# A decoder layer on one core: the rotary halves of the token totals are mixed before the token sum, by GpSimd and VectorE, instead of after it, by TensorE

## The chip, the cores and the metric

The kernel runs on one core of one Trainium2 chip. The metric is device time in microseconds; the figure compared is a median of several runs. The core has a matrix engine (TensorE, PE in the profile, with its weight loads shown apart as PEld), VectorE (DVE), ScalarE (ACT), GpSimd (POOL) and SyncE (SP), which only issues transfers. The engines run their own instruction streams in order and meet at semaphores.

## The reference, cut to what matters

The program is one decoder layer over 4 batches of 512 tokens and 512 features: an attention-like block, a second product with a context, and a feed-forward block with experts. The part that the change touches is in the first block:

```
Xn = layernorm(X) * gamma + beta
Q, K, V = split(Xn @ W_in + b_in)                 # 512 features each
K, V = rotary(K), rotary(V)                       # on the first 256 features
A = sum over tokens of (K/|K|) * (V/|V|)          # one vector of 512 per batch
Y = (0.5 * A + 0.5) * Q                           # the same A for every token
out = Y @ W_out + b_out + X
```

The rotation turns neighbouring features (2m, 2m+1) into each other. The product of a rotated K and a rotated V, element by element, is for a pair: half the sum of the two plain products, plus or minus half of a term that contains the cosine and sine of twice the angle. So a plain product and a "rotated" term are summed over the tokens, and the pair is mixed once per batch instead of once per token.

## The kernel before, in words

The program has two stages. The first (up to about 211 us of the profile) makes K, V, Q, the vector A and the attention output of the four batches, then one maximum over everything; the second does the context product and the feed-forward part. The change is in the first stage.

Every large product in it is done as three products of split numbers (high times high, high times low, low times high), of 512 columns each. Per batch b of the first stage TensorE's order, written out by hand, is: K and V of the four token tiles 0 to 3 (`key_value`, lines 898 to 928; each of the four steps k of a tile is six products at lines 908 and 914), four query products c = 0 to 3 of 12 matmuls (`query`, lines 864 to 866) with transposes of the next batch between them, and the four attention output tiles of the batch before (`attention`). After batch 3 there are the attention tiles of batch 2, then query 0 to 3 of batch 3 (line 1065), and the attention tiles of batch 3. Queries 0 and 2 write the same PSUM bank, as do 1 and 3: query(b, c) for c of 2 or 3 waits until ScalarE has copied query(b, c - 2) out (line 954).

The token totals. For each token tile VectorE adds a bias to K and V (`add_kv_bias`, lines 640 and 641), ScalarE sums squares (line 418), GpSimd makes a weight from them (`weight`, lines 319 and 321), and VectorE forms five products (`products`, lines 657 to 665): 512 plain ones and 256 rotated ones. Tile 0 writes them into `total` (128 x 768), the others into `prod`, and GpSimd starts a transfer that adds `prod` to `total` (line 328). In the last batch VectorE does the last of these additions itself (`last_total`, line 671). Before products(b, 0) overwrites `total`, it waits until the token sum of batch b - 1 is done (line 654).

The token sum and the mixing. TensorE sums `total` over its 128 partitions with six small products against a column of ones (line 940), two or three at a time between the steps of other products: for batch 0 after the first and the second step of K/V tile 2 of batch 1 (line 1036), for batches 1 and 2 after the third and the fourth step of K/V tile 1 of the next batch (line 1029), for batch 3 within query 2 (line 965). ScalarE copies the six columns out (`copy_sums`, line 424), and three more small products against constant matrices mix the pairs (`mix_sums`, lines 948 to 950): ahead of K/V tile 3 of the next batch, in batch 3 inside query 3. VectorE makes the multiplier `amul` from that (line 675), ScalarE makes the high half of Y with it (`high_y`, line 441), VectorE the low half (`low_y`, line 681).

VectorE's order in batch b = 1 is: add_kv_bias(1, 0), next_stats(2), ctx_amax(1), add_kv_bias(1, 1), products(1, 0), normalise of batch 2, add_kv_bias(1, 2), products(1, 1), ctx_amax(2), multiplier(0), low_y(0, 0 to 3), add_kv_bias(1, 3), products(1, 2) and (1, 3). ScalarE's is: the squares of tiles 0 and 1, copy_sums(0), the squares of tile 2, high_y(0, 0 to 3), query(1, 0), query(1, 1), the squares of tile 3, query(1, 2).

Of the kernel before, what the change touches and what calls it, by code (L numbers as in the profile page):

```python
# [23 lines left out]
P = 128  # L24
B, S, D = 4, 512, 512
KC = D // P
CHUNKS = (D + D // 2) // P
# [23 lines left out]
C_ID, C_MIX, C_IOTA, C_TRIG = 0, P, 4 * P, 4 * P + TOPK  # L51
# [3 lines left out]
def shape_constants():  # L55

    c = np.zeros((P, C_ALL), np.float32)
    c[:, C_ID:C_ID + P] = np.eye(P)
    i = np.arange(P)
    pair = (i[:, None] // 2 == i[None, :] // 2).astype(np.float64)  # L60
    even = (i % 2 == 0)
    c[:, C_MIX:C_MIX + P] = 0.5 * pair
    c[:, C_MIX + P:C_MIX + 2 * P] = np.where(np.eye(P) > 0, 0.5, -0.5 * pair)
# [27 lines left out]
def decoder_layer(nc, x, ctx, mask, w_in, b_in, w_out, b_out, gamma, beta, w_q, keys, down_embed, up_embed,  # L91
# [14 lines left out]
    with ExitStack() as whole:  # L106
# [57 lines left out]
        with ExitStack() as first:  # L164
# [18 lines left out]
            mix = sb("mix", [P, 2, P], F32)  # L183
# [8 lines left out]
            ones_col = sb("ones_col", [P, 1], F32)  # L192
            rsum = sb("rsum", [P, 8], F32)
# [18 lines left out]
            total_all, total_in, rsum_done, mix_mm, amul_done = sem("total_all"), sem("total_in"), sem("rsum_done"), sem("mix_mm"), sem("amul_done")  # L212
# [39 lines left out]
            def _(sp):  # L252
# [17 lines left out]
                sp.dma_start(mix[:].rearrange("p a b -> p (a b)"), consts[:, C_MIX:C_MIX + 2 * P]).then_inc(s_const, 16)  # L270
# [21 lines left out]
            def _(pool):  # L292
# [3 lines left out]
                nc.gpsimd.memset(ones_col[:], 1.0).then_inc(s_pool_const, 1)  # L296
                nc.gpsimd.memset(ones_sq[:], 1.0).then_inc(s_pool_const, 1)
                pool.wait_ge(s_pool_const, 4)
# [75 lines left out]
            def _(act):  # L374
# [45 lines left out]
                def copy_sums(b):  # L420
                    act.wait_ge(asum_mm, b + 1)
                    if b:
                        act.wait_ge(mix_mm, b)
                    nc.scalar.activation(rsum[:, 0:6], ob[0][:, 0:6], ACT.Copy).then_inc(rsum_done, 1)

# [39 lines left out]
                for b in range(B):  # L465
# [59 lines left out]
                copy_sums(LAST)  # L525
# [16 lines left out]
            def _(dve):  # L542
# [319 lines left out]
            def _(pe):  # L862
# [67 lines left out]
                def token_sums(b, chunks):  # L930

                    if b == LAST:
                        pe.wait_ge(z_done, TB * (b - 1) + 3)
                    if b == LAST:
                        pe.wait_ge(total_all, 1)
                    else:
                        pe.wait_ge(total_in, 16 * 3 * (b + 1))
                        pe.wait_ge(prod_done, TB * b + 1)
                    for c in chunks:
                        last = nc.tensor.matmul(ob[0][:, c:c + 1], total[:, c * P:(c + 1) * P], ones_col[:], start=(c == 0), stop=(c == CHUNKS - 1), skip_group_check=True)  # L940
                    if c == CHUNKS - 1:
                        last.then_inc(asum_mm, 1)

                def mix_sums(b):
                    if b == LAST:
                        pe.wait_ge(z_done, TB * (b - 1) + 4)
                    pe.wait_ge(rsum_done, b + 1)
                    nc.tensor.matmul(ob[1][:, 0:2], mix[:, 0], rsum[:, 0:2], start=True, stop=False, skip_group_check=True)
                    nc.tensor.matmul(ob[1][:, 0:2], mix[:, 1], rsum[:, 4:6], start=False, stop=False, skip_group_check=True)
                    nc.tensor.matmul(ob[1][:, 2:4], ident[:], rsum[:, 2:4], start=False, stop=True, skip_group_check=True).then_inc(mix_mm, 1)  # L950

                def query(b, c, sums=None, mix_of=None):
# [10 lines left out]
                    for k in range(KC):  # L963
                        if sums is not None and k:
                            token_sums(sums, range(2 * k - 2, 2 * k))
                        if mix_of is not None and k == 1:
                            mix_sums(mix_of)
# [3 lines left out]
                def attention(b, i):  # L971
# [5 lines left out]
                    elif i >= 2:  # L977
                        pe.wait_ge(*((rsum_done, b + 1), (amul_done, b + 1))[i - 2])
# [41 lines left out]
                pe.wait_ge(s_const, 32)  # L1020
                pe.wait_ge(s_pool_const, 4)
                for b in range(B):
                    if b:
                        first_key_value(b)
                        for i in range(1, 2):
                            for k in range(KC):
                                key_value(b, i, k)
                                if b > 1 and k >= 2:
                                    token_sums(b - 1, range(3 * (k - 2), 3 * (k - 1)))
# [9 lines left out]
                    if b:  # L1039
# [28 lines left out]
                query(LAST, 3, mix_of=LAST)  # L1068
# [25 lines left out]
        with ExitStack() as second:  # L1094
# [199 lines left out]
            def _(pool):  # L1294
                own = Steps(pool, s_psteps)
                own.base, own.n = 0, TB * B
# [783 lines left out]
```

## Time and profile before

| what | value |
|---|---|
| time, median of 3 runs | 791.81 us (791.77 to 791.91) |
| span of the profiled execution, first to last instruction | 789.7 us |
| TensorE busy | 774.6 us, 98% of the span |
| VectorE busy | 663.4 us, 84% |
| ScalarE busy | 322.7 us, 41% |
| GpSimd busy | 357.4 us, 45% |
| mean granted TensorE clock | 0.997 |

The profile shows one execution. Of that execution its span is given, and no time of its own beside it; the span lies 2.1 us under the median of the runs. Rows of a timeline give start in us, duration in us, engine, line, operation, output and inputs with shapes, a count of merged instructions, and in brackets how long the engine had been idle before and what released it. A float32 product that is not in the split form counts as two matmuls (the six small products of a token sum show as x12).

### The profile page before, as it was taken

The numbers are of one execution on the slowest core, as the hardware profiler recorded it, in microseconds if no ns is written. First come the engines' busy times: TensorE is split into PE (matmuls) and PEld (weight loads), VectorE is DVE, ScalarE is ACT, GpSimd is POOL, SyncE is SP. The second block draws the span as 40 slices with busy tenths as digits, with TensorE's granted clock in tenths as the row PEclk, the third lists the DMA queues.
The fourth block names the chain that finished last, engine by engine and source line by source line (L and its number), as shares of the span: only waits on it lengthen the run. The fifth ranks groups of instructions, "written<-read, shape, count | busy, mean of one in ns | idle before, by whom it ended". The sixth has DMA issues, their size and how long they took to land.

```text
span 789.7 us, 10694 instructions
## 1 busy us (share of the span) xinstructions
PE 774.6 (98%) x3590; PEld 637.1 (81%) x3590; DVE 663.4 (84%) x1346; ACT 322.7 (41%) x704; POOL 357.4 (45%) x308
## 2 busy tenths in 40 slices
PE   8999999999899999999999999999999999999996
PEld 7888888887667778888888888888888888888885
DVE  6888679998898870476779998999999999899875
ACT  6444336456574422222443433334333343343314
POOL 1241222242122411014476676776776677676323
PEclk9999999999999999999999999999999999999998
DMA  8666504624454528001122231431333224242013
GB/s 321 249 131 164 94 5 101 169 79 76 79 143 110 158 84 289 1 1 32 60 70 79 82 89 40 127 95 46 93 114 106 87 79 119 60 132 55 16 63 150
DMA packets 51046, 79.92 MB, mean 101 GB/s; under 512 B 17487, under 2 KB 26447, under 8 KB 50480
## 3 DMA queue, kind: packets, MB, share of 16 engines
q0 software_dynamic: 24240, 31.52, 18.6%
q1 hardware_dynamic: 25168, 47.72, 17.2%
q8 instruction: 28, 0.46, 0.2%
q10 hardware_dynamic: 1584, 0.01, 0.1%
q14 instruction: 26, 0.21, 0.1%
HBM read 110.64 MB, written 12.58 MB: 156 GB/s over the span
## 4 chain that ended last, share of the span: by engine, by line
PE 64%; DVE 4%; issue 2%; POOL 2%; ACT 1%; POOLq 0%; DVEq 0%; ACTq 0%
PE gu L1870 14%; PE gu L1871 14%; PE gu L1869 14%; PE ob L1947 6%; PE ob L1943 6%; PE ob L1942 6%; DVE scratch L1566 1%; DVE scratch L1568 1%; POOL h_lo L1306 1%; DVE x_lo L1613 1%; PE gu L2041 0%; PE ob L1896 0%; ACT junk L1443 0%; DVE xall L1607 0%; PE ob L1963 0%
## 5 line engine op out<-in xcount | busy, mean ns | idle before, releaser
L1869 PE MATMUL gu<-x_hi,w_hi 128*128 128x512 f32 x516 | 201.4, 390 | 0.0
L1871 PE MATMUL gu<-x_hi,w_lo 128*128 128x512 f32 x516 | 200.8, 389 | 0.0
L1870 PE MATMUL gu<-x_lo,w_hi 128*128 128x512 f32 x516 | 200.7, 389 | 0.0
L1306 POOL TENSOR_TENSOR h_lo<-mid,h_hi 128x512 fp32r<-128x512 f32 x62 | 86.8, 1417 | 176.0 <-ACT h_hi L1455 176.0
L1871 PEld LDWEIGHTS gu<-x_hi,w_lo 128*128 128x128 f32 x516 | 96.8, 188 | 20.1
L1869 PEld LDWEIGHTS gu<-x_hi,w_hi 128*128 128x128 f32 x516 | 96.9, 188 | 20.1
L1870 PEld LDWEIGHTS gu<-x_lo,w_hi 128*128 128x128 f32 x516 | 96.9, 188 | 19.9
L1465 ACT ACTIVATE gates<-dots 128x1 f32<-128x1 f32 x144 | 29.2, 203 | 175.3 <-DVE dots L1715 175.3
L1624 DVE TENSOR_TENSOR mid<-gu,mid 128x512 f32<-128x512 f32 x64 | 44.0, 687 | 66.4 <-PE gu L1871 56.5
L1942 PE MATMUL ob<-w_hi,h_hi 128*128 128x512 f32 x224 | 87.1, 389 | 0.0
L1943 PE MATMUL ob<-w_lo,h_hi 128*128 128x512 f32 x224 | 87.1, 389 | 0.0
L1325 POOL DMA_INDIRECT ctx_q<-table_dram,row_i x64 | 73.6, 1150 | 18.8 <-issue 17.0
L1325 POOL DMA_INDIRECT scratch<-table_dram,row_i x64 | 73.1, 1141 | 16.5 <-issue 15.0
L1455 ACT ACTIVATE h_hi<-mid 128x512 fp32r<-128x512 f32 x62 | 36.2, 625 | 85.4 <-PE ob L1947 62.4
L1947 PE MATMUL ob<-w_hi,h_lo 128*128 128x512 f32 x224 | 69.0, 389 | 0.0
L1449 ACT ACTIVATE mid<-gu 128x512 f32<-128x512 f32 x64 | 37.8, 591 | 63.4 <-PE gu L1871 54.8
L1787 DVE TENSOR_TENSOR xall<-ob,xall 128x512 f32<-128x512 f32 x94 | 59.4, 684 | 3.6 <-PE ob L1947 1.6
L1301 POOL TENSOR_TENSOR w_lo<-xhat,w_hi 128x1024 fp32r<-128x1024 f32 x21 | 50.4, 2399 | 24.1 <-ACT w_hi L1419 15.9
L1715 DVE CUSTOM_DVE_ANT_0 junk<-x_tok,ctx_q 128x512 bf16<-128x512 f32 x64 | 60.4, 944 | 0.5
L1724 DVE SCALAR_TENSOR_TENSOR xall<-ctx_q,coef,xall 128x512 f32<-128x512 f32 x64 | 60.1, 939 | 0.0
L1724 DVE SCALAR_TENSOR_TENSOR xall<-scratch,coef,xall 128x512 f32<-128x512 f32 x64 | 59.6, 931 | 0.0
L1715 DVE CUSTOM_DVE_ANT_0 junk<-x_tok,scratch 128x512 bf16<-128x512 f32 x64 | 57.2, 893 | 0.3
(254 smaller groups left out, 1431.0 us busy)
## 6 DMA issues: line engine op xcount, KB each, us to landing
stage<-in_ctx SPq DMA_DIRECT2D x7, 1024.0 KB, 5.6
total<-prod POOLq DMA_DIRECT2D x11, 384.0 KB, 4.3
xall<-half_bo POOLq DMA_DIRECT2D x4, 1024.0 KB, 9.2
xhat<-in_L_ffn_gate_w SPq DMA_DIRECT2D x8, 512.0 KB, 3.5
xhat<-in_L_ffn_up_w SPq DMA_DIRECT2D x8, 512.0 KB, 3.7
xall<-in_mask_Bx1xS_ff POOLq DMA_DIRECT2D x4, 1024.0 KB, 10.4
xhat<-in_L_ffn_down_w SPq DMA_DIRECT2D x8, 512.0 KB, 3.6
x_dram<-xall SPq DMA_DIRECT2D x4, 1024.0 KB, 6.7
```

The costliest lines, as they stand in the source:

```text
L1301: nc.gpsimd.tensor_tensor(flat(lo, r), stage_of(r, slot), flat(hi, r).bitcast(F32), ALU.subtract).then_inc(wlo_done, 1)
L1306: nc.gpsimd.tensor_tensor(lo[:, c], mid[c][:], hi[:, c].bitcast(F32), ALU.subtract).then_inc(hlo_done, 1)
L1325: nc.gpsimd.indirect_dma_start(rows[k], None, table_dram[:, :], bass.IndirectOffsetOnAxis(ap=row_i[t % 2][:, k:k + 1], axis=0), bounds_che ...
L1715: nc.vector.tensor_tensor_reduce(out=junk2[:], in0=x2_tok[par][:], in1=row[:, 0:D], scale=1.0, scalar=0.0, op0=ALU.mult, op1=ALU.add, accu ...
L1724: nc.vector.scalar_tensor_tensor(tile(t), row[:, D:2 * D], coef[:, t % 2, k:k + 1], tile(t), ALU.mult, ALU.add).then_inc(pick_done, 1)
L1787: nc.vector.tensor_tensor(tile(j), ob[i][:], tile(j), ALU.add).then_inc(acc_done, 1)
L1869: nc.tensor.matmul(dst, lhs[0], rhs[0], start=start, stop=False)
L1870: nc.tensor.matmul(dst, lhs[0], rhs[1], start=False, stop=False)
L1871: return nc.tensor.matmul(dst, lhs[1], rhs[0], start=False, stop=stop)
L1942: nc.tensor.matmul(ob[i][:], h[0][:, c, ts], w_high[:, c], start=(c == 0), stop=False)
L1943: nc.tensor.matmul(ob[i][:], h[0][:, c, ts], w_low[:, c], start=False, stop=False)
L1947: last = nc.tensor.matmul(ob[i][:], h[1][:, c, ts], w_high[:, c], start=False, stop=(c == GC - 1))
```

## The change

`mix_sums`, `copy_sums`, the constant matrices and their load are removed. A new function mixes the pairs in `total` itself, ahead of the token sum: GpSimd does it for batches 0 to 2, VectorE for batch 3, inside `last_total`. TensorE then sums four blocks instead of six; the first two with a column of 0.5. The token sum of batch 0 moves from K/V tile 2 to K/V tile 3 of batch 1; that of batch 3 stands as one group of four ahead of the last step of query 2. The multiplier waits for the token sum directly.

```diff
+                def mix_total(b):
+
+                    pool.wait_ge(total_in, 16 * 3 * (b + 1))
+                    plain, turned = total[:, 0:ROT], total[:, D:D + ROT]
+                    own.did(nc.gpsimd.tensor_tensor(apart[:], plain, turned, ALU.subtract))
+                    own.did(nc.gpsimd.tensor_tensor(plain, plain, turned, ALU.add))
+                    own.wait()
+                    nc.gpsimd.tensor_tensor(plain.rearrange("p (n t) -> p n t", t=2), plain.rearrange("p (n t) -> p n t", t=2),
+                                            apart[:].rearrange("p (n t) -> p n t", t=2)[:, :, ::-1], ALU.add).then_inc(total_mixed, 1)
...
                 for b in range(B):
                     if b >= 2:
+                        mix_total(b - 1)
                         z_rstd(b - 2)
                     weight(b, 0)
                     if b < LAST:
                         x_rstd(part_of(b + 1))
+                    if b == 1:
+                        mix_total(0)
                     weight(b, 1)
...
-                    if b:
-                        copy_sums(b - 1)
-                    else:
+                    if b == 0:
                         high_wo()
...
-                    nc.vector.tensor_tensor(total[:], total[:], prod[:, (TB - 1) % 2], ALU.add).then_inc(total_all, 1)
+                    own.did(nc.vector.tensor_tensor(total[:], total[:], prod[:, (TB - 1) % 2], ALU.add))
+                    own.wait()
+                    plain, turned = total[:, 0:ROT], total[:, D:D + ROT]
+                    dve.wait_ge(total_mixed, LAST)
+                    own.did(nc.vector.tensor_tensor(apart[:], plain, turned, ALU.subtract))
+                    own.did(nc.vector.tensor_tensor(plain, plain, turned, ALU.add))
+                    own.wait()
+                    nc.vector.tensor_tensor(plain.rearrange("p (n t) -> p n t", t=2), plain.rearrange("p (n t) -> p n t", t=2),
+                                            apart[:].rearrange("p (n t) -> p n t", t=2)[:, :, ::-1], ALU.add).then_inc(total_mixed, 1)
...
                 def multiplier(b):
-                    dve.wait_ge(mix_mm, b + 1)
-                    nc.vector.tensor_scalar(amul[:], ob[1][:, 0:KC], 0.5, 0.5, ALU.mult, ALU.add).then_inc(amul_done, 1)
+                    dve.wait_ge(asum_mm, b + 1)
+                    nc.vector.tensor_scalar(amul[:], ob[0][:, 0:KC], 0.5, 0.5, ALU.mult, ALU.add).then_inc(amul_done, 1)
...
-                    if b == LAST:
-                        pe.wait_ge(total_all, 1)
-                    else:
-                        pe.wait_ge(total_in, 16 * 3 * (b + 1))
-                        pe.wait_ge(prod_done, TB * b + 1)
+                    pe.wait_ge(total_mixed, b + 1)
                     for c in chunks:
-                        last = nc.tensor.matmul(ob[0][:, c:c + 1], total[:, c * P:(c + 1) * P], ones_col[:], start=(c == 0), stop=(c == CHUNKS - 1), skip_group_check=True)
+                        halved = 0 if c * P < ROT else 1
+                        last = nc.tensor.matmul(ob[0][:, c:c + 1], total[:, c * P:(c + 1) * P], sum_cols[:, halved:halved + 1], start=(c == 0), stop=(c == KC - 1), skip_group_check=True)
...
                                 if b > 1 and k >= 2:
-                                    token_sums(b - 1, range(3 * (k - 2), 3 * (k - 1)))
+                                    token_sums(b - 1, range(2 * (k - 2), 2 * (k - 1)))
...
                     for k in range(KC):
                         key_value(b, 2, k)
-                        if b == 1 and k < 2:
-                            token_sums(b - 1, range(3 * k, 3 * k + 3))
                     if b == 2:
                         spread()
-                    if b:
-                        mix_sums(b - 1)
                     for k in range(KC):
                         key_value(b, 3, k)
+                        if b == 1 and k < 2:
+                            token_sums(b - 1, range(2 * k, 2 * k + 2))
```

## Rows read from the trace of the kernel before

**Rows 1.** The page: busy time of each engine.
```profile
PE 774.6 (98%) x3590; PEld 637.1 (81%) x3590; DVE 663.4 (84%) x1346; ACT 322.7 (41%) x704; POOL 357.4 (45%) x308
```

**Rows 2.** Timeline of VectorE, batch 1: products of tile 0 and multiplier.
```profile
62.29 0.75 DVE L657 SCALAR_TENSOR_TENSOR total<-kv,wgt 128x512 f32<-128x512 f32 x1 [1.13 <-PE ob L940]
...
72.14 0.15 DVE L675 TENSOR_SCALAR amul<-ob 128x4 f32<-128x4 f32 x1
```

**Rows 3.** Timeline of ScalarE, batch 1: high half of Y, query 0 copied out.
```profile
72.39 2.56 ACT L441 ACTIVATE y_hi<-qT,amul 128x512 fp32r<-128x512 f32 x4 [3.16 <-DVE amul L675]
74.86 0.67 ACT L433 ACTIVATE qT<-ob,b_q 128x512 f32<-128x512 f32 x1
```

**Rows 4.** Timeline of TensorE, batch 1: K/V tiles 2 and 3, later query 2.
```profile
58.02 0.62 PE L908 MATMUL gu<-w_hi,xn_hi 128*128 128x512 f32 x2
...
59.38 0.72 PE L940 MATMUL ob<-ones_col,total 128*128 128x1 f32 x6
59.96 0.71 PE L908 MATMUL gu<-w_hi,xn_hi 128*128 128x512 f32 x2
...
61.43 0.72 PE L940 MATMUL ob<-ones_col,total 128*128 128x1 f32 x6
62.02 0.71 PE L908 MATMUL gu<-w_hi,xn_hi 128*128 128x512 f32 x2
...
63.48 0.62 PE L908 MATMUL gu<-w_hi,xn_hi 128*128 128x512 f32 x2
...
65.43 0.71 PE L908 MATMUL gu<-w_hi,xn_hi 128*128 128x512 f32 x2
...
76.42 0.39 PE L864 MATMUL ob<-xn_hi,w_hi 128*128 128x512 f32 x1
```

**Rows 5.** Timeline of TensorE, batch 3: two steps of query 2 with token sums.
```profile
184.28 0.48 PE L864 MATMUL ob<-xn_hi,w_hi 128*128 128x512 f32 x1
...
185.43 0.47 PE L864 MATMUL ob<-xn_hi,w_hi 128*128 128x512 f32 x1
```

**Rows 6.** Timeline of VectorE, batch 2: bias of tile 1, residual of tile 1.
```profile
106.33 0.69 DVE L640 TENSOR_TENSOR kv<-gu,b_kv 128x512 f32<-128x512 f32 x1 [1.84 <-PE gu L914]
...
139.01 0.68 DVE L687 SCALAR_TENSOR_TENSOR xall<-xall,ob 128x512 f32<-128x512 f32 x1
```

**Rows 7.** Stretches at the end: length, busy per engine, PEclk, DMA share, GB/s.
```profile
783.00:784.00 1.00, 0.28 (x2) 0.00 (x0) 1.00 (x2) 1.00 (x3) 0.62 (x2) 1.00 0.00 0
...
785.00:785.50 0.50, 0.00 (x0) 0.00 (x0) 0.20 (x2) 0.00 (x0) 0.19 (x1) 0.94 0.72 270
```

**Rows 8.** Timeline of TensorE, batch 2: first product of attention tile 3.
```profile
139.81 0.44 PE L864 MATMUL ob<-wo_hi,y_hi 128*128 128x512 f32 x1
```

**Rows 9.** Timeline of VectorE, batch 3, from the last products to the last residual.
```profile
178.69 0.42 DVE L663 TENSOR_TENSOR crossed<-crossed,trig 128x256 f32<-128x256 f32 x1
...
182.74 0.96 DVE L671 TENSOR_TENSOR total<-total,prod 128x768 f32<-128x768 f32 x1
183.62 2.28 DVE L597 SCALAR_TENSOR_TENSOR stage<-stage 128x2048 f32<-128x2048 bf16 x1
...
190.03 0.16 DVE L675 TENSOR_SCALAR amul<-ob 128x4 f32<-128x4 f32 x1 [0.33 <-PE ob L950]
...
204.91 0.69 DVE L687 SCALAR_TENSOR_TENSOR xall<-xall,ob 128x512 f32<-128x512 f32 x1 [0.31 <-PE ob L866]
```

**Rows 10.** Timeline of GpSimd: a total's last transfer, two reciprocal roots of 128x4.
```profile
53.88 0.90 POOL L328 DMA_DIRECT2D total<-prod  x1 [6.16 <-DVE prod L665]
...
57.86 1.02 POOL L304 TENSOR_TENSOR rstd<-var_eps,neg_half 128x4 f32<-128x4 f32 x1 [0.51 <-DVE var_eps L556]
...
144.92 3.00 POOL L334 TENSOR_TENSOR rstd<-var,neg_half 128x4 f32<-128x4 f32 x1 [7.48 <-DVE var L697]
```

**Rows 11.** The page: a GpSimd subtraction of two tiles, and landing of the totals' transfers.
```profile
L1306 POOL TENSOR_TENSOR h_lo<-mid,h_hi 128x512 fp32r<-128x512 f32 x62 | 86.8, 1417 | 176.0 <-ACT h_hi L1455 176.0
...
total<-prod POOLq DMA_DIRECT2D x11, 384.0 KB, 4.3
```

More of the change, by code:

```diff
@@ L26 @@
 KC = D // P
-CHUNKS = (D + D // 2) // P
 NT = B * S // P
@@ L48 @@
 IDLE_PRODUCTS = 16
-C_ID, C_MIX, C_IOTA, C_TRIG = 0, P, 4 * P, 4 * P + TOPK
+C_ID, C_IOTA, C_TRIG = 0, P, P + TOPK
 C_ALL = C_TRIG + TB * 3 * P
@@ L59, in shape_constants @@
     i = np.arange(P)
-    pair = (i[:, None] // 2 == i[None, :] // 2).astype(np.float64)
     even = (i % 2 == 0)
-    c[:, C_MIX:C_MIX + P] = 0.5 * pair
-    c[:, C_MIX + P:C_MIX + 2 * P] = np.where(np.eye(P) > 0, 0.5, -0.5 * pair)
     c[:, C_IOTA:C_IOTA + TOPK] = np.arange(TOPK)
@@ L182, in decoder_layer @@
             trig = sb("trig", [P, TB, 3 * P], F32)
-            mix = sb("mix", [P, 2, P], F32)
             b_kv = sb("b_kv", [P, 2 * D], F32)
@@ L191, in decoder_layer @@
             wgt = sb("wgt", [P, 2, 1], F32)
-            ones_col = sb("ones_col", [P, 1], F32)
-            rsum = sb("rsum", [P, 8], F32)
+            sum_cols = sb("sum_cols", [P, 2], F32)
+            apart = sb("apart", [P, ROT], F32)
             amul = sb("amul", [P, KC], F32)
@@ L211, in decoder_layer @@
             kv_mm, kv_out, sq_done, wgt_ready, prod_done, asum_mm = (sem(n) for n in ("kv_mm", "kv_out", "sq_done", "wgt_ready", "prod_done", "asum_mm"))
-            total_all, total_in, rsum_done, mix_mm, amul_done = sem("total_all"), sem("total_in"), sem("rsum_done"), sem("mix_mm"), sem("amul_done")
+            total_in, total_mixed, amul_done = sem("total_in"), sem("total_mixed"), sem("amul_done")
             qt_mm, qt_out, yhi_done, ylo_done = sem("qt_mm"), sem("qt_out"), sem("yhi_done"), sem("ylo_done")
@@ L269, in _ @@
                 sp.dma_start(half_bo[:], b_out.partition_broadcast(P)).then_inc(hb_in, 16)
-                sp.dma_start(mix[:].rearrange("p a b -> p (a b)"), consts[:, C_MIX:C_MIX + 2 * P]).then_inc(s_const, 16)
                 sp.dma_start(iota8[:], consts[:, C_IOTA:C_IOTA + TOPK]).then_inc(s_const, 16)
@@ L295, in _ @@
                 nc.gpsimd.memset(ones_row[:], 1.0).then_inc(s_pool_const, 1)
-                nc.gpsimd.memset(ones_col[:], 1.0).then_inc(s_pool_const, 1)
+                nc.gpsimd.memset(sum_cols[:, 0:1], 0.5).then_inc(s_pool_const, 1)
+                nc.gpsimd.memset(sum_cols[:, 1:2], 1.0).then_inc(s_pool_const, 1)
                 nc.gpsimd.memset(ones_sq[:], 1.0).then_inc(s_pool_const, 1)
-                pool.wait_ge(s_pool_const, 4)
+                pool.wait_ge(s_pool_const, 5)
                 def x_rstd(p):
@@ L418, in squares @@
                         nc.scalar.activation(junk[:], kv[:, i % 2, which], ACT.Square, accum_out=norm2[:, i % 2, which:which + 1]).then_inc(sq_done, 1)
-                def copy_sums(b):
-                    act.wait_ge(asum_mm, b + 1)
-                    if b:
-                        act.wait_ge(mix_mm, b)
-                    nc.scalar.activation(rsum[:, 0:6], ob[0][:, 0:6], ACT.Copy).then_inc(rsum_done, 1)
                 def query(b, c):
@@ L524, in _ @@
                     scale_x1(LAST - 1, i)
-                copy_sums(LAST)
                 query(LAST, 2)
@@ L933, in token_sums, with query @@
                         pe.wait_ge(z_done, TB * (b - 1) + 3)
-                    if b == LAST:
-                        pe.wait_ge(total_all, 1)
-                    else:
-                        pe.wait_ge(total_in, 16 * 3 * (b + 1))
-                        pe.wait_ge(prod_done, TB * b + 1)
+                    pe.wait_ge(total_mixed, b + 1)
                     for c in chunks:
-                        last = nc.tensor.matmul(ob[0][:, c:c + 1], total[:, c * P:(c + 1) * P], ones_col[:], start=(c == 0), stop=(c == CHUNKS - 1), skip_group_check=True)
-                    if c == CHUNKS - 1:
+                        halved = 0 if c * P < ROT else 1
+                        last = nc.tensor.matmul(ob[0][:, c:c + 1], total[:, c * P:(c + 1) * P], sum_cols[:, halved:halved + 1], start=(c == 0), stop=(c == KC - 1), skip_group_check=True)
+                    if c == KC - 1:
                         last.then_inc(asum_mm, 1)
[L944 to L952, printed above, removed]
+                def query(b, c, sums=None):
                     if c >= 2:
@@ L963, in query @@
                     for k in range(KC):
[L964 to L967, printed above, removed]
+                        if sums is not None and k == KC - 1:
+                            token_sums(sums, range(KC))
                         last = three(ob[2 + c % 2][:], w_hi[:, k, c * P:(c + 1) * P], w_lo[:, k, c * P:(c + 1) * P], xn_hi[:, k], xn_lo[:, k], k == 0, k == KC - 1)
@@ L977, in attention @@
                     elif i >= 2:
-                        pe.wait_ge(*((rsum_done, b + 1), (amul_done, b + 1))[i - 2])
+                        pe.wait_ge(amul_done, b + 1)
+                        if b == LAST and i == 3:
+                            pe.wait_ge(z_done, TB * LAST)
                     elif b == LAST:
@@ L1019, in _ @@
                             key_value_low(0, i, k - 1)
-                pe.wait_ge(s_const, 32)
-                pe.wait_ge(s_pool_const, 4)
+                pe.wait_ge(s_const, 16)
+                pe.wait_ge(s_pool_const, 5)
                 for b in range(B):
@@ L1067, in _ @@
                 query(LAST, 2, sums=LAST)
-                query(LAST, 3, mix_of=LAST)
+                query(LAST, 3)
                 pe.wait_ge(x1_done, TB)
@@ L1295, in _ @@
                 own = Steps(pool, s_psteps)
-                own.base, own.n = 0, TB * B
+                own.base, own.n = 0, TB * B + 2 * (B - 1)
                 def low_w(m, g_set, r, slot):
```

1 line of the change is left out of this document (removed).

## The prediction

> **What bounds the kernel now.** I read the page first: TensorE is busy 98% of the span [rows 1], so a product taken out of its stream is worth its whole length, if nothing else holds the stream up at that place. That condition is the question here. The change takes small products out of TensorE's stream, but it also moves one token sum to a later place, and three other engines hang on token sums. So I read the timelines of TensorE, VectorE and ScalarE beside each other around each place, looking for idle time of VectorE that ends with a token sum, and for rows of VectorE that follow each other without a gap.
>
> In batch 1 VectorE waits 1.13 us for the token sum of batch 0 and starts products(1, 0) at 62.29 [rows 2]. From there to the multiplier at 72.14 it has 15 rows and no idle time in any. ScalarE has idled 3.16 us when that multiplier releases high_y, 2.56 us of work, and right behind it it copies query(1, 0) out from 74.86, which takes 0.67 us [rows 3]. That copy frees the bank for query(1, 2), which TensorE begins at 76.42 [rows 4]. So one chain runs from the token sum to query(1, 2), and all its slack is 76.42 - 75.53 = 0.9 us.
>
> **What TensorE saves.** A K/V step (six products) without small products takes 59.38 - 58.02 = 1.36 us, four of them 5.44; right behind a small group it takes 63.48 - 62.02 = 1.46 us. With a group of three token blocks a step and its group take 62.02 - 59.96 = 2.06 us, so a group costs 0.70 us [rows 4]. The mixing products cost (65.43 - 63.48) - 1.36 = 0.59 us, and 0.10 us more of the step behind them: 0.70 us too [rows 4]. A group of two blocks costs 185.43 - 184.28 = 1.15 us less the 0.68 us of three plain matmuls (half of the 1.36 us of six), 0.47 us [rows 5]. Batches 0 to 2 each had 2 x 0.70 + 0.70 = 2.10 us and get 2 x 0.47 = 0.94 us: 1.16 us less on TensorE's stream per batch, 3.5 us in all.
>
> **What the moved sum costs.** The sum of batch 0 went from K/V tile 2 to tile 3. After the change tile 2 runs bare from 58.02 to 63.46; the first step of tile 3 and its group of two end the 1.83 us later, at 65.29; the second step ends near 66.65 and its group is over at 67.15. VectorE started 0.14 us after the end of the second group before (61.43 + 0.72 = 62.15, against 62.29), so now it starts products(1, 0) at 67.29: 5.0 us later [rows 2, 4]. Every step of the chain is in order and without a gap, so the copy of query(1, 0) ends at 75.53 + 5.0 = 80.5. TensorE, which has 1.16 us less to do, wants to begin query(1, 2) at 75.26. It idles 5.3 us there, and begins 80.55 - 76.42 = 4.1 us later than before. The 1.16 us of batch 0's sum is inside this number: it only makes the wait longer. Behind that wait stand all of TensorE's later products; the rest of the batch follows them, since VectorE waits for TensorE again at the next batch (1.84 us idle [rows 6]). Nothing returns the 4.1 us.
>
> **What an idle TensorE costs besides.** At the very end TensorE is busy for the last time at 783.28 (0.28 us of the microsecond from 783), and the granted clock is full until the stretch from 785.0 to 785.5, whose mean 0.94 says that it fell from the 2.4 to the 1.2 GHz level near 785.44: after 2.2 us of idleness [rows 7]. No idle time before that is as long. One of 5.3 us is over twice as long, so I take it that the clock falls inside it and that query(1, 2) begins at 1.2 GHz. No matmul of this trace runs at that level, so the price is bounded: nothing if the clock is back at once, 2.7 us (12 matmuls, twice the 1.36 us of six) if the whole of query(1, 2) takes twice its time. I take the middle, 1.4 us. The Trainium skill has the same in TensorE: Matmul & The Clock Gate, section HAM oscillation: a wait between bursts of matmuls lets the engine fall back to half rate, and the next burst starts slow; the trace agrees as far as the fall goes [rows 7], and no row of it shows the return.
>
> **Batches 2 and 3.** The token sum stays where it was, one block shorter per group. VectorE's work in batch 2 hangs on the end of K/V tile 1 (1.84 us idle, 106.33), and is then nearly unbroken to the residual of tile 1 at 139.01, which ends 139.69; TensorE's attention tile 3 needs it and begins at 139.81 with a product of 0.44 us instead of 0.39 [rows 6, 8]. The slack there is 0.1 us. Of the 1.16 us saved only one shorter group, 0.23 us, lies before 106.33 and moves VectorE too; the other 0.9 us become a wait of TensorE. I count 0.2 us gained for batch 2. In batch 3 VectorE has almost no idle time to the end of the stage, so TensorE's gain there moves nothing: zero (bounds: 0 and 1.16).
>
> **The last token total.** VectorE mixes it itself: three operations of 128x256. Such an operation takes 0.42 us and one starts every 0.34 to 0.46 [rows 9]; three add 1.25 us between 182.74 and ctx_quantise. At 190.03 the multiplier had waited 0.33 us for the mixing products, and the residual of the last tile 0.31 us for TensorE [rows 9]; TensorE is done sooner at both places now, so both waits go: 1.25 - 0.33 - 0.31 = +0.6 us at the end of the stage. TensorE's own savings here (three groups to one, the mixing, 0.99 us of wait for ScalarE's copy) lie beside VectorE's path and are worth nothing.
>
> **GpSimd.** mix_total is not in the trace. A 128x512 subtraction takes 1.42 us [rows 11], a half as wide one 0.7 us by proportion and at most the 1.42: three take 2.1 to 4.3 us. For batch 0 the last transfer starts at 53.88 and lands 4.3 us later, and a root at 57.86 ends at 58.88 [rows 10, 11]. The total is mixed at 61.0 to 63.2, ahead of the 64.8 at which TensorE now wants it. For batches 1 and 2 the sum stands behind seven K/V steps of the next batch (9.5 us), and the last transfer is started before these: enough for the 4.3 us of landing and even 4.3 us of mixing. Cost zero. The loads and copies that are dropped were on nobody's path: zero.
>
> **The sum.** 4.1 + 1.4 - 0.2 + 0.6 = +5.9 us. The profiled execution has a span of 789.7 us, 2.1 under the median; the sum is of differences, so the span would be 795.6 and the median 791.81 + 5.9 = 797.7 us.
>
> **Rivals.** (a) The clock does not fall, or returns at once. Then the sum is +4.5 us, 796.3. For it: one fall at the end of a program is thin evidence for the middle of one. Against it: the gap is over twice 2.2 us. Chance 0.30. (b) The wait for query 2 does not come about, and the kernel is faster. The place is query(1, 2), the price is the 4.1 + 1.4 us, and it decides when VectorE gets to products(1, 0) less than 0.9 us late, or catches up as much. TensorE then keeps 1.16 us of batch 0's sum and 0.2 to 2.3 of the others, less 0.6 at the end: -0.8 to -2.9, in the middle 790.0. Against it stand 15 rows without a gap; what could do it is a wait that the code spells more strictly than the chip meets it. Chance 0.07. (c) GpSimd's mixing of batch 0 comes late as well. One root took 3.00 us beside a VectorE operation, its like 1.02 [rows 10]. If the three operations take 3 us each, the total is mixed at 67.9 instead of by 64.8, the token sum and VectorE are 3.1 us later again, and the time is about 800.8. Against it: VectorE is idle from 61.2 on [rows 2], so there is nothing beside them. The Trainium skill, SBUF — State Buffer, section SBUF: two separate sides, states that VectorE and GpSimd take turns at a shared pair of ports for whole instructions; the 3.00 against 1.02 us fits. Chance 0.06. (d) The stall comes but nearly all that is saved later on is kept (TensorE is the bound of batches 2 and 3 after all, 1.16 each instead of 0.2, and the clock stays): 4.1 - 2.3 + 0 = +1.8, 793.6. Chance 0.05.
>
> **How the numbers follow.** My forecast has 0.52, and rivals (a) 0.30, (b) 0.07, (c) 0.06, (d) 0.05. The range from 794.6 to 799.4 holds the forecast with its clock price between 0 and 2.7 and rival (a) with half of (d)'s savings. Faster by over 0.2% (1.6 us, about what a measurement tells from no change) is most of (b): 0.06. Within 0.2% is the rest of (b) and the lower side of (d): 0.04. Slower is 0.90.
>
> **What would show it.** In the changed kernel's TensorE timeline, query(1, 2) has some 5 us of idle time before it, ended by ScalarE's copy; in VectorE's, products(1, 0) starts at 67.3 behind some 6 us of idle time, ended by the token sum; the clock is under 1 around 80 us; in batch 2 attention tile 3 starts behind a new short wait for VectorE; the stage ends near 217 instead of 211. If TensorE goes from query(1, 1) to query(1, 2) without a gap, the prediction is wrong at its main step.

## The result, and the profile after

The changed kernel takes 797.56 us, median of 4 runs (796.54 to 798.52), against 791.79 for the kernel before: ratio 1.007, 95% interval 1.0058 to 1.0083. It is 5.8 us slower; the prediction said 797.7. The profiled execution is the longest of the four, 798.52 us, with a span of 796.7, 7.0 us more than before, so its rows add up to 7.0 and not to 5.8.

The page of the changed kernel, busy time and granted clock in 40 slices, answers to [rows 1]:

```profile
PE 775.5 (97%) x3546; PEld 634.7 (80%) x3550; DVE 664.4 (83%) x1349; ACT 322.2 (40%) x700; POOL 362.7 (46%) x318
...
PEclk9999899999999999999999999999999999999999
```

TensorE's row has 44 matmuls fewer (the code removes 40, as many as weight loads are gone; four more are missing among the records) and is busy 0.9 us longer: some of its matmuls ran at the lower clock, in the slice with the 8 (around 80 to 100 us) above all. Now the same three timelines. TensorE in batch 1, the late token sum and query(1, 2), beside [rows 4]:

```profile
64.89 0.50 PE L944 MATMUL ob<-sum_cols,total 128*128 128x1 f32 x4
...
66.74 0.50 PE L944 MATMUL ob<-sum_cols,total 128*128 128x1 f32 x4
...
80.66 0.79 PE L871 MATMUL ob<-xn_hi,w_hi 128*128 128x512 f32 x1 [5.14 <-ACT qT L435]
81.25 0.63 PE L872 MATMUL ob<-xn_lo,w_hi 128*128 128x512 f32 x1
...
85.94 1.24 PE L899 MATMUL ob<-ident,xhat 128*128 128x128 f32 x8
```

VectorE, beside [rows 2]:

```profile
67.38 0.75 DVE L656 SCALAR_TENSOR_TENSOR total<-kv,wgt 128x512 f32<-128x512 f32 x1 [6.18 <-PE ob L944]
...
77.22 0.15 DVE L682 TENSOR_SCALAR amul<-ob 128x4 f32<-128x4 f32 x1
```

ScalarE, beside [rows 3], where the two copies of queries now stand together:

```profile
77.47 2.56 ACT L443 ACTIVATE y_hi<-qT,amul 128x512 fp32r<-128x512 f32 x4 [3.15 <-DVE amul L682]
79.94 1.24 ACT L435 ACTIVATE qT<-ob,b_q 128x512 f32<-128x512 f32 x2
```

The reader is to see one chain moved whole: the sum ends 5.1 us later, VectorE's 6.18 us of idle time end with it, the multiplier comes 5.1 us later, ScalarE behind it too, and TensorE's 5.14 us of idle time end with ScalarE's copy. query(1, 2) begins 4.24 us later than before, and its 12 matmuls need 5.28 us (80.66 to 85.94) instead of 2.7.

The clock, in stretches (length, TensorE's busy time, PEclk, DMA share, GB/s). A PEclk between 0.50 and 1.00 is the mean of a stretch in which the clock changed between its two levels, and tells at what point it did:

```profile
77.00:78.00 1.00, 0.00 (x0) 1.00 1.06 197
78.00:79.00 1.00, 0.00 (x0) 1.00 1.33 197
79.00:80.00 1.00, 0.00 (x0) 0.77 0.43 141
80.00:81.00 1.00, 0.34 (x1) 0.50 1.03 401
...
85.00:86.00 1.00, 1.00 (x4) 0.50 0.00 0
86.00:88.00 2.00, 2.00 (x14) 0.91 1.00 184
```

The clock falls to 1.2 GHz at 79.54, 4.0 us after TensorE stopped (75.13 + 0.39 = 75.52), and is back at 2.4 GHz at 86.36 (the 0.91 over 2 us is 0.36 us at the lower level), 5.7 us after TensorE went on at 80.66.

Further on, VectorE in batches 2 and 3, beside [rows 6] and [rows 9]:

```profile
113.10 0.69 DVE L639 TENSOR_TENSOR kv<-gu,b_kv 128x512 f32<-128x512 f32 x1 [1.64 <-PE gu L921]
...
145.77 0.68 DVE L694 SCALAR_TENSOR_TENSOR xall<-xall,ob 128x512 f32<-128x512 f32 x1
...
189.08 0.96 DVE L670 TENSOR_TENSOR total<-total,prod 128x768 f32<-128x768 f32 x1
190.07 0.43 DVE L674 TENSOR_TENSOR apart<-total 128x256 f32<-128x256 f32 x1
190.42 0.42 DVE L675 TENSOR_TENSOR total<-total 128x256 f32<-128x256 f32 x1
190.87 0.42 DVE L677 TENSOR_TENSOR total<-total,apart 128x256 f32<-128x256 f32 x1
191.21 2.28 DVE L596 SCALAR_TENSOR_TENSOR stage<-stage 128x2048 f32<-128x2048 bf16 x1
...
196.93 0.15 DVE L682 TENSOR_SCALAR amul<-ob 128x4 f32<-128x4 f32 x1
...
211.06 0.68 DVE L694 SCALAR_TENSOR_TENSOR xall<-xall,ob 128x512 f32<-128x512 f32 x1
...
218.14 0.16 DVE L1730 TENSOR_TENSOR unscale<-scale_x,scale_c 128x1 f32<-128x1 f32 x1 [1.30 <-PEq L160]
```

TensorE's attention tiles 2 and 3 in batch 2, and below them VectorE's residual of tile 0. The new short wait stands ahead of tile 2, for that residual (142.78 + 0.68 = 143.46); tile 3, the tile of [rows 8], starts at 146.50, right behind the end of the residual of tile 1 (145.77 + 0.68 = 146.45):

```profile
143.51 0.50 PE L871 MATMUL ob<-wo_hi,y_hi 128*128 128x512 f32 x1 [0.36 <-DVE xall L694]
...
146.50 0.50 PE L871 MATMUL ob<-wo_hi,y_hi 128*128 128x512 f32 x1
```
```profile
142.78 0.68 DVE L694 SCALAR_TENSOR_TENSOR xall<-xall,ob 128x512 f32<-128x512 f32 x1
```

Subtracting the rows of before gives the lag of the changed kernel from place to place: 4.24 at query(1, 2), 6.77 at the bias of batch 2's tile 1, 6.76 at the residual at 145.77, 6.34 at the last total, 6.90 at the multiplier, 6.15 at the last residual, and 6.94 at the first row of the second stage (211.20 before). At the end of the program it is 7.0: over the second stage as a whole nothing is gained or lost.

### The profile page after: what moved, and what is told of

The parts are those of the page before. It is cut to its first block, busy times and chain, and to the rows that moved or that the text cites. A ratio compares the mean times of both kernels' runs of the same rounds, so it can differ in the third digit from the quotient of the medians.

```text
span 796.7 us, 10608 instructions
## 1 busy us (share of the span) xinstructions
PE 775.5 (97%) x3546; PEld 634.7 (80%) x3550; DVE 664.4 (83%) x1349; ACT 322.2 (40%) x700; POOL 362.7 (46%) x318
## 4 chain that ended last, share of the span: by engine, by line
PE 64%; DVE 4%; issue 2%; POOL 2%; ACT 1%; POOLq 0%; DVEq 0%; ACTq 0%
PE gu L1863 14%; PE gu L1864 14%; PE gu L1865 14%; PE ob L1937 6%; PE ob L1936 6%; PE ob L1941 6%; DVE scratch L1560 1%; DVE scratch L1562 1%; POOL h_lo L1300 1%; DVE x_lo L1607 1%; PE gu L2035 0%; PE ob L1890 0%; ACT junk L1437 0%; DVE xall L1601 0%; PE ob L1957 0%
```

## The experiments

My theory was the prediction's: the late token sum holds VectorE at products(1, 0), and so TensorE at query(1, 2); the idle TensorE loses its clock; the savings in batches 2 and 3 are lost to VectorE. The main rival was that the new mixing itself, on GpSimd or VectorE, makes the loss.

**Token sum of batch 0 earlier, nothing else.**

```diff
                     for k in range(KC):
                         key_value(b, 2, k)
+                        if b == 1 and k == 2:
+                            token_sums(b - 1, range(KC))
...
                         key_value(b, 3, k)
-                        if b == 1 and k < 2:
-                            token_sums(b - 1, range(2 * k, 2 * k + 2))
```

> The changed kernel with one thing moved: the token sum of batch 0 stands as one group of four blocks behind the third step of K/V tile 2 of batch 1, the first place behind the end of GpSimd's mixing (61.2 us). Theory (the late token sum makes the loss, through products(1, 0)): the sum is over near 63.0, VectorE starts products(1, 0) at 63.2 instead of 67.4, TensorE's wait ahead of query(1, 2) shrinks from 5.1 to 1.1 us, the clock does not fall there, query(1, 2) begins at 76.4 as in the kernel before. Time 791.0, up to 791.9 if the clock falls at the end of the first stage as it did in the profile of the changed kernel. Rival (the loss is in GpSimd's mixing or its ports, or in VectorE's three operations of the last batch): these are all still there, so the time stays near 797.5.

Measured: 791.19 us (ratio to the kernel before 0.9994, interval 0.9985 to 1.0003). VectorE and TensorE in its timelines:

```profile
63.38 0.75 DVE L656 SCALAR_TENSOR_TENSOR total<-kv,wgt 128x512 f32<-128x512 f32 x1 [2.01 <-PE ob L944]
```
```profile
76.67 0.50 PE L871 MATMUL ob<-xn_hi,w_hi 128*128 128x512 f32 x1 [1.02 <-ACT qT L435]
```

With all of the mixing in place the loss is gone. The wait of 1.02 us takes nearly what TensorE saved. The rival falls.

**The kernel before, with only its token sum moved to the late place.**

```diff
-                        if b == 1 and k < 2:
-                            token_sums(b - 1, range(3 * k, 3 * k + 3))
...
-                    if b:
+                    if b > 1:
                         mix_sums(b - 1)
                     for k in range(KC):
                         key_value(b, 3, k)
+                        if b == 1 and k < 2:
+                            token_sums(b - 1, range(3 * k, 3 * k + 3))
+                    if b == 1:
+                        mix_sums(b - 1)
```

> The kernel before, with nothing of the mixing changed: only the token sum of batch 0 is moved behind the first and second step of K/V tile 3 of batch 1, and its mixing products behind that tile. Theory: VectorE starts products(1, 0) 5.3 us later (67.6), TensorE, which saves nothing here, waits 4.4 us ahead of query(1, 2) and begins it 4.5 us late; the clock falls in that wait, 2.6 us more: 798.9, and 796.3 if it does not fall. Rival (the loss comes from the new mixing, not from the place of the sum): 791.8, no change.

Measured: 799.17 us (ratio 1.0084, interval 1.0070 to 1.0097). VectorE starts products(1, 0) at 67.93, and TensorE's row is:

```profile
81.21 0.80 PE L864 MATMUL ob<-xn_hi,w_hi 128*128 128x512 f32 x1 [4.44 <-ACT qT L433]
```

The place of the sum alone makes the whole loss, and more, since here nothing is saved. Its clock fell in the wait as well (0.76 in the microsecond from 80, so at 80.5, 3.7 us after TensorE stopped). Its five executions lie in two groups: three at 799.17 to 799.44 with a mean clock of 0.993 or 0.994, and two at 797.96 and 798.04 with 0.997.

**TensorE kept busy during the wait.**

```diff
                     query(b, 1)
+                    if b == 1:
+                        pe.wait_ge(kv_out, TB + 3)
+                        for _ in range(42):
+                            nc.tensor.transpose(gu[0][:, 0:P], ident[:], ident[:])
                     query(b, 2)
```

> The changed kernel, with 42 transposes of the identity that nobody reads ahead of query(1, 2) of batch 1 (4.8 us at 0.114 each), so that TensorE is busy while it would wait. Theory (the fallen clock is a price of its own, about 2.6 us in the profiled run): query(1, 2) begins at 80.7 as in the changed kernel but its 12 matmuls take 2.7 us instead of 5.3, time 795.2, up to 796.1 if the clock falls at the end of the first stage. Rival (the wait alone is the price, the low clock lies in slack): 797.5, no change from the changed kernel.

Measured: 795.34 us (ratio 1.0045, interval 1.0031 to 1.0058), 2.2 less than the changed kernel. Its timeline of TensorE, and two stretches of all engines (the clock stands third from the end):

```profile
75.36 4.75 PE L1046 MATMUL gu<-ident 128*128 128x128 f32 x42
80.67 0.50 PE L871 MATMUL ob<-xn_hi,w_hi 128*128 128x512 f32 x1 [0.56 <-ACT qT L435]
...
83.53 1.04 PE L899 MATMUL ob<-ident,xhat 128*128 128x128 f32 x8
```
```profile
80.00:82.00 2.00, 1.44 (x7) 1.12 (x7) 2.00 (x4) 1.19 (x3) 0.00 (x0) 1.00 0.99 367
82.00:84.00 2.00, 2.00 (x13) 1.66 (x12) 1.97 (x5) 1.72 (x5) 0.00 (x0) 1.00 0.27 103
```

query(1, 2) begins at 80.67, as before the edit (80.66), and takes 2.86 us; the five microseconds from 75 have a clock of 1.00 too. The clock is a price of its own, on top of the wait.

**Two buffers for the totals.** The odd batches write theirs into a part of `stage[0]` that is free by then.

```diff
+            totals = [total[:], stage[0][:, 2 * D:3 * D + ROT]]
...
-                    if b:
-                        dve.wait_ge(asum_mm, b)
+                    if b and i:
+                        dve.wait_ge(total_in, 16 * 3 * b)
+                    elif b >= 2:
+                        dve.wait_ge(asum_mm, b - 1)
```

> The changed kernel with two buffers for the totals, one for even and one for odd batches, so that products(b, 0) waits for the sum of batch b - 2 and products(b, 1 to 3) for the transfers of batch b - 1; the token sum of batch 0 stays late. Theory (the wait of products(1, 0) is the only thing through which the late sum costs): products(1, 0) starts at 61.2, no wait ahead of query(1, 2), TensorE keeps the 1.16 us of batch 0's sum and 0.2 of batch 1's, and some 0.6 us of small waits on VectorE's path in batch 3: 789.8, up to 790.7 with a fall of the clock at the end of the first stage. Rival (the multiplier itself, which waits for the sum too, or the moved products on TensorE make the loss): 795 or more.

Measured: 790.15 us (ratio to the kernel before 0.9978, interval 0.9969 to 0.9987). VectorE goes on at once:

```profile
61.27 0.75 DVE L659 SCALAR_TENSOR_TENSOR stage<-kv,wgt 128x512 f32<-128x512 f32 x1
```

TensorE has no wait ahead of query(1, 2), with the sum in its late place. So the late sum costs only through products(1, 0). Of its 11 executions nine are at 789.9 to 790.2 and two at 790.85 and 791.04.

**The last batch unmixed, on top of two buffers.** VectorE's three operations are left out of `last_total`, so the last batch's sums are not mixed.

```diff
-                    own.did(nc.vector.tensor_tensor(apart[:], plain, turned, ALU.subtract))
-                    own.did(nc.vector.tensor_tensor(plain, plain, turned, ALU.add))
...
```

> The kernel with two buffers for the totals, without VectorE's three mixing operations in the last batch (they are left out, so the last batch's sums are not mixed). Theory (these three cost 1.25 us less the two waits that they fill, 0.6 us, as the prediction had it): 789.5 against the 790.15 of the kernel with two buffers. Rival from the profile of the changed kernel (VectorE's small waits behind them swallow all of the 1.25 us): 790.1, no change.

Measured: 789.05 us (ratio 0.9969, interval 0.9957 to 0.9980), 1.1 less than with them. The two intervals overlap, but six of its seven executions (788.93 to 789.51; the seventh took 790.01) are below the shortest of the kernel with two buffers, 789.90. They cost most of their 1.25 us: both costs that I gave, 0.6 and nothing, were too low.

**Batch 2 lighter on VectorE, on top of two buffers.** The four normalisations of batch 0 are left out; those rows are not normalised.

```diff
                     dve.wait_ge(rstd2_ready, b + 1)
-                    own.did(nc.vector.tensor_scalar(tile(j), tile(j), mv2[:, i, 0:1], rstd2[:, i:i + 1], ALU.subtract, ALU.mult))
-                    own.wait()
+                    if b:
+                        own.did(nc.vector.tensor_scalar(tile(j), tile(j), mv2[:, i, 0:1], rstd2[:, i:i + 1], ALU.subtract, ALU.mult))
+                        own.wait()
```

> The kernel with two buffers for the totals, without the four subtractions and scalings of batch 0's rows that VectorE does in batch 2 between K/V tile 1 and the residuals (4 x 0.58 us, left out, so the values of batch 0 are not normalised there; the maxima are still taken). Theory (in batch 2 TensorE's 0.9 us of saving is lost because attention tile 3 waits for VectorE's residual): that wait goes and TensorE keeps 0.9 us: 789.2 against 790.15. Rival (VectorE bounds the rest of the stage too, or the saving is lost elsewhere): 790.1, or more than 0.9 less if VectorE's whole path in batch 3 was the bound (2.3 us less, 787.8).

Measured: 789.04 us (ratio 0.9965, interval 0.9951 to 0.9978), 1.1 less; all five executions are between 788.96 and 789.15. The kernel with two buffers has this row, at attention tile 2 again, and the lighter one has no idle time of TensorE in that stretch:

```profile
135.71 0.50 PE L874 MATMUL ob<-wo_hi,y_hi 128*128 128x512 f32 x1 [0.39 <-DVE xall L697]
```

So VectorE's path holds back TensorE's saving of batch 2, and of the 2.3 us taken from it only that saving comes out.

**The end of the first stage filled.** In the profile of the changed kernel the clock also falls, at 216.06 (0.53 in the microsecond from 216), behind 1.10 us and then 0.54 us of idle time of TensorE. Two kernels have 17 instead of 8 transposes there, one with two buffers, one the changed kernel as it is.

```diff
                 pe.wait_ge(z_done, NT)
-                keep_running(8)
+                keep_running(17)
```

> The kernel with two buffers for the totals, with 17 instead of 8 transposes of the identity after the last residual, so that TensorE's 1.1 us of idle time at the end of the first stage are filled. Theory (the clock falls in some executions because of that idle time, which costs those about 0.9 us): no execution near 791.0 any more, all near 790.0. Rival (the falls have another cause): the same spread as before, 789.9 to 791.0.

Measured: 789.92 us (ratio 0.9975, interval 0.9966 to 0.9984), all executions between 789.73 and 790.07. None of the 11 is near 791; without this edit two of 11 were, which is too few to call the difference shown, and no trace of one of those two was taken. This is the fastest version that computes the layer, by a hair.

> The changed kernel with 17 instead of 8 transposes of the identity after the last residual, so that TensorE's 1.1 us of idle time at the end of the first stage are filled; the wait ahead of query(1, 2) stays. Theory (the spread of the changed kernel, 796.5 to 798.5, is two falls of the clock: one certain, ahead of query(1, 2), whose length varies, and one at the end of the stage in some executions): the upper ones go, 796.5 to 797.7, and the profile shows one stretch at 1.2 GHz of some 6.6 us around 80 us and none at 216. Rival (the second fall follows from the first or is by chance): the spread stays and the profile shows a second stretch.

Measured: 797.38 us (796.99 to 798.07; ratio 1.0071, interval 1.0058 to 1.0085). Two of the five executions, 797.92 and 798.07, are above the range that I gave. The profiled one, 798.07, has the stretch around 80 us and none at 216:

```profile
79.00:80.00 1.00, 0.00 (x0) 0.00 (x0) 1.00 (x3) 1.00 (x3) 0.00 (x0) 0.77 0.59 107
...
216.00:218.00 2.00, 1.45 (x12) 1.21 (x12) 0.98 (x6) 0.28 (x1) 0.29 (x1) 1.00 0.00 0
```

The second fall is absent here, and the stretch from the last residual to the second stage takes 6.28 us (211.47 to 217.75), as in the kernel before (6.29) and not 7.08 as in the changed kernel: that is its price, 0.8 us. The first fall is the same in both profiles (79.54 to 86.36). Yet this execution lasts only 0.45 us less than the profiled one of the changed kernel, because ScalarE waits for a transfer of the context in batch 3, and that transfer came 0.4 us later here. The changed kernel, and below it this one:

```profile
161.46 2.01 ACT L454 ACTIVATE stage<-stage,scale_c 128x2048 f32<-128x2048 f32 x1 [2.63 <-DMA stage<-in_ctx]
```
```profile
161.87 2.01 ACT L454 ACTIVATE stage<-stage,scale_c 128x2048 f32<-128x2048 f32 x1 [2.98 <-DMA stage<-in_ctx]
```

VectorE is 0.40 us later from there to the last residual. So the spread of the changed kernel (2.0 us, here 1.1) has at least three sources, the first fall, the second one and this transfer, and the runs do not say how much each has.

**The kernel before with two buffers.** The edit is that of the two buffers, applied to the kernel before.

> The kernel before with two buffers for the totals and nothing else. Theory (there VectorE's wait for the token sum lay in slack, TensorE bounds that stretch): 791.7, no change, though VectorE starts products(1, 0) at 61.2 instead of 62.3. Rival (the buffers alone make the kernel with two buffers faster): 790.2.

Measured: 791.79 us (ratio 1.0003, interval 0.9994 to 1.0012). The 1.13 us of [rows 2] lay in slack. The 1.6 us of the version with two buffers are gained by the mixing and the buffers together: the buffers alone give nothing, and the mixing with an early sum gave 0.5, within its interval.

**The last batch mixed by GpSimd**, on top of two buffers and 17 transposes, with the token sum one query later.

```diff
                 last_z_rstd(slice(0, TB))
+                mix_total(LAST)
                 add_mask(0)
```

> The kernel with two buffers and 17 transposes, with the mixing of the last batch on GpSimd too, behind its reciprocal roots, and the token sum of the last batch ahead of the last step of query 3 instead of query 2. Theory (VectorE's path is the bound there and GpSimd has time): its three operations take 0.74 us each, the total is mixed some 2.5 us after VectorE's last addition, ahead of the sum, and VectorE is 1.25 us earlier as without mixing: 788.9 against 789.92. Rival (GpSimd is held up by VectorE's two long operations that follow right there, as its root of 3.00 us beside such an operation was): the three end 4.5 us after the addition or later, the sum and the multiplier wait for them, 790 or more.

Measured: 791.83 us (ratio 1.0005, interval 0.9996 to 1.0014), 1.9 slower than without this edit. GpSimd, and below it VectorE and the token sum on TensorE:

```profile
182.54 3.02 POOL L371 TENSOR_TENSOR rstd<-var,neg_half 128x4 f32<-128x4 f32 x1
185.55 2.03 POOL L333 TENSOR_TENSOR apart<-stage 128x256 f32<-128x256 f32 x1
187.55 0.71 POOL L334 TENSOR_TENSOR stage<-stage 128x256 f32<-128x256 f32 x1
188.35 0.72 POOL L336 TENSOR_TENSOR stage<-stage,apart 128x256 f32<-128x256 f32 x1
```
```profile
182.39 2.29 DVE L601 SCALAR_TENSOR_TENSOR stage<-stage 128x2048 f32<-128x2048 bf16 x1
184.71 2.29 DVE L603 SCALAR_TENSOR_TENSOR ctx_q<-stage 128x2048 bf16<-128x2048 bf16 x1
...
190.28 0.16 DVE L681 TENSOR_SCALAR amul<-ob 128x4 f32<-128x4 f32 x1 [1.81 <-PE ob L943]
```
```profile
189.21 1.02 PE L943 MATMUL ob<-sum_cols,stage 128*128 128x1 f32 x8 [2.73 <-POOL stage L336]
```

The rival held: the root ends at 185.56 and the first subtraction at 187.58, 0.9 and 0.6 us behind the ends of VectorE's two long operations (184.68 and 187.00), and the total is mixed 6.6 us after its last addition (182.47), not 2.5. The token sum waits for GpSimd, the multiplier for the token sum. Three of its 11 executions took 793.45 to 793.59, in spite of the 17 transposes, as single executions of the kernel before do (4 of 21 beside the first experiments at 792.3 to 793.4): the 17 transposes do not take away every slower execution.

## Why the prediction was right

**The moved sum (+4.1).** Right in place, mechanism and size: products(1, 0) at 67.38 (forecast 67.29), query(1, 2) at 80.66 (80.55), 4.24 us late. Shown from both sides: moving the sum back removes the loss, moving it in the kernel before makes it, and a second buffer makes its place harmless.

**The clock (+1.4).** Right that it falls, too small for the profiled execution: the lag goes from 4.24 to 6.80 us over query(1, 2) and to 7.00 over the transposes behind it (79.94 before, 86.94 after), 2.8 us, the upper bound and a little more, since the clock came back only behind the whole of query(1, 2). Over the runs it is less: 797.56 - 795.34 = 2.2 us, or 2.0 with the 17 transposes at the end of the stage (797.38). Rival (a) is refuted for the profiled executions. In three kernels with the late sum the executions with a mean clock of 0.997 are also the shortest (796.54; 796.99; 797.96 and 798.04), so a shorter or missing low stretch is likely there. A shorter one exists: in the profile of the last batch unmixed the clock is low for 3.4 us (211.4 to 214.9), in the others for 6.8. But no trace of one of the short executions was taken, and that stays open.

**Batch 2 (-0.2).** Right: 6.97 at the start of its K/V (94.56 before, 101.53 after), 6.77 from tile 1 on, and the lighter VectorE gives the lost 0.9 back (1.1 in the median). The place was not quite the one that I named: TensorE's lag is 5.91 us at attention tile 1 (134.27 before, 140.18 after), 6.42 at tile 2 (137.09, 143.51), where I had seen no wait since VectorE's residual of tile 0 was 0.4 us early before, and 6.69 at tile 3. Rival (d), which had these savings kept, did not come up; its sum also leaves out the +0.6 of the last total without a reason.

**Batch 3 (0).** Off by 0.4: the lag goes from 6.76 to 6.34 us. Two waits that I had read as fixed parts of VectorE's path shrank, the one of its ctx_quantise for ScalarE (0.50 us from the row ahead, 158.33 to 158.83, before; 0.35, 165.10 to 165.45, after) and the one between multiplier and low_y (1.28 us before, 164.56 to 165.84; 0.99 after, 171.19 to 172.18). The first hangs on the context transfer shown above and is scatter of the execution: in the changed kernel with 17 transposes VectorE's lag there is 7.02 us. Why ScalarE begins high_y sooner behind the multiplier in the second, the profile does not say.

**The last total (+0.6).** The step that was mis-sized. Mixing adds the 1.25 us that I had (183.62 to 191.21 is 7.59, against a lag of 6.34), and leaving it out gives 1.1 of it back. But behind it the lag falls by 1.44, to 6.15, and not by the 0.64 of two waits. Counted from start to start of VectorE's rows the two waits are worth 0.41 us each, and three more that I had passed over went as well: 0.27 ahead of the multiplier, where VectorE waited for ScalarE (189.02 before), 0.12 at the last low_y and 0.20 at the residual of tile 2 (202.18 before). The 0.27 are filled by VectorE being later, since they come back when the last batch is left unmixed (there VectorE idles 0.20 us at the same place); the rest does not come back there, so it goes with TensorE and ScalarE being earlier, for which the missing mixing products and copy are the likely reason. Net -0.2.

**The end of the stage (not in the prediction).** TensorE is ahead of VectorE there by more than before, idles 1.10 instead of 0.41 us, its clock falls in this execution, and the transposes that end the stage hold up the switch to the second: 6.94 against 6.13, +0.8. In the execution without this fall nothing is lost there (6.28 us against 6.29 before).

**GpSimd (0).** Right, though not for the reason that I gave against rival (c). The three operations took 0.73, 0.73 and 0.74 us, and the total of batch 0 was mixed at 61.2, ahead of 64.9. But VectorE was not idle beside them: they ran before 61.2, and like the root of 1.02 us ahead of them partly beside a long operation of VectorE, a maximum over one input. GpSimd, and below it VectorE:

```profile
57.90 1.02 POOL L299 TENSOR_TENSOR rstd<-var_eps,neg_half 128x4 f32<-128x4 f32 x1 [0.51 <-DVE var_eps L555]
58.91 0.73 POOL L329 TENSOR_TENSOR apart<-total 128x256 f32<-128x256 f32 x1
```
```profile
57.73 2.28 DVE L591 TENSOR_REDUCE amax_c<-stage 128x1 f32<-128x2048 f32 x1
```

The roots of 3.00 and 3.02 us ran beside a scalar_tensor_tensor of 2.28 or 2.29 us instead. So the mechanism of rival (c) is real, as the last experiment shows, but the kind of operation that VectorE runs matters, and not only whether it is busy. The Trainium skill (SBUF — State Buffer, section SBUF: two separate sides) has it that a VectorE operation with two inputs in SBUF and a GpSimd operation that reads SBUF take turns for whole instructions. The trace agrees on GpSimd's side; VectorE's long operations kept their 2.29 us.

The profiled execution sums to 4.2 + 2.8 - 0.2 - 0.4 - 0.2 + 0.8 = 7.0 us, all of it. That the median came within 0.2 us of the forecast is partly luck: the clock was under by 0.6 to 1.4, the end of the stage was missing, batch 3 gave 0.4 that were not forecast, and the last total was over by 0.8.

## What to carry to other kernels

Before moving a small product to a later place on a saturated TensorE, look who waits for it elsewhere: here VectorE had idle time of only 1.1 us ended by it, but 15 rows without a gap and two more engines behind it, and 0.9 us of slack at the end of that chain against a move of 5. Products taken out of TensorE are only worth their length where nothing comes back from the other engines just in time; where that is so, the saved time turns into a wait, and a wait can cost the clock besides. Work that moves to GpSimd has to be checked against the kind of operation that VectorE runs at that time. A second buffer for the thing waited for was worth more than the choice of the place.

## What the runs showed of the hardware that I had not expected

The lower clock outlasted its cause: after 5.14 us of idle time TensorE ran another 5.7 us at 1.2 GHz, so a wait of 5 us cost 2.8 us more. The fall itself came after different idle times: 2.2 us at the end of the kernel before, 3.7 and 4.0 us in the two kernels with the late sum. The clock also fell around the end of the first stage with two short idle times, 1.10 to 1.13 us and 0.54 us, close together and small transposes between, in two profiles (the changed kernel and the last batch unmixed) and not in four others with the same idle times. It did not fall there in the three with nine more transposes, nor in the three with 0.41 us in place of the 1.10. What decides between the two and the four, no run here shows. In the changed kernel that fall cost 0.8 us. Transposes of the identity, 42 in 4.75 us, were enough to keep the clock at 2.4 GHz. And GpSimd's root of 128x4, 1.02 us beside a VectorE maximum of 2.28 us over one input, took 3.02 us beside a scalar_tensor_tensor of 2.29 us, and 1.28 us where VectorE ran mostly short operations.
